# Elementwise work of a fused attention kernel, moved from VectorE to ScalarE and GpSimd

## The reference

```
x1 = x  + a_alpha * attention(ada(x))                        # 16 heads of 16
x2 = x1 + f_alpha * (silu(h @ gate) * (h @ hidden) @ out + out_b)   # h = ada(x1), hidden width 1024
u  = (x2 * scale * rsqrt(mean(x2^2) + eps)) @ up             # second layer
y  = int8_quant(val * gelu(gate)) @ ternary(down) + x2
```

## Time and profile before

| what | us |
|---|---|
| median of 3 runs | 1106.18 (1102.67 to 1108.35) |
| the profiled execution | 1105.27 |
| its span in the trace | 1103.5 |
| TensorE busy | 1032.5 (94%) |
| VectorE busy | 775.7 (70%) |
| ScalarE busy | 562.2 (51%) |
| GpSimd busy | 345.8 (31%) |

### The profile page before, as it was taken

The page is one execution under the profiler, slowest core; times in us unless marked ns, Lnnn a source line. Parts: engine busy times, 40 slices in busy tenths (PEclk is TensorE's granted clock), DMA queues, the critical chain, the costliest instruction groups (busy, mean ns, idle before and its releaser), DMA issues.

```text
span 1103.5 us, 19199 instructions
## 1 busy us (share of the span) xinstructions
PE 1032.5 (94%) x6775; PEld 719.0 (65%) x6775; DVE 775.7 (70%) x1557; ACT 562.2 (51%) x1260; POOL 345.8 (31%) x414
## 2 busy tenths in 40 slices
PE   7788799999999999999999999979989999899997
PEld 6233357746765775677577557734868888788775
DVE  5777686687669667857875786676647787466775
ACT  5357574567566555756665575555552323132221
POOL 2410142423333332324233242201332444243331
PEclk9799999999999999999999999998999999999998
DMA  8644623154153406423440623160310111002111
GB/s 265 155 99 152 93 91 122 17 102 149 59 86 98 142 2 112 126 87 48 117 141 21 112 87 107 28 142 1 97 53 29 59 58 30 29 29 63 59 53 39
DMA packets 89375, 92.71 MB, mean 84 GB/s; under 512 B 11856, under 2 KB 86616, under 8 KB 88256
## 3 DMA queue, kind: packets, MB, share of 16 engines
q1 hardware_dynamic: 87248, 89.59, 31.1%
q10 hardware_dynamic: 2032, 1.90, 0.6%
HBM read 61.68 MB, written 29.78 MB: 83 GB/s over the span
## 4 chain that ended last, share of the span: by engine, by line
PE 77%; DVE 13%; issue 5%; DMA 2%; POOL 1%; ACT 1%; SPq 0%; POOLq 0%; DVEq 0%; ACTq 0%
PE gen L1171 30%; PE core L1171 13%; PE pvb L1286 11%; PE core L1260 9%; PE core L1274 8%; DVE negmax L932 7%; PE gen L1498 2%; PE gen L1245 1%; PE pvb L1490 1%; DVE o L956 1%; PE pvb L1294 1%; DMA parts_d<-qk 1%; DMA shift_d<-shift 1%; PE gen L1324 1%; PE core L1264 1%
## 5 line engine op out<-in xcount | busy, mean ns | idle before, releaser
L932 DVE TENSOR_REDUCE negmax<-core 128x1 f32<-128x512 f32 x512 | 338.1, 686 | 166.4 <-PE core L1260 165.2
L715 ACT ACTIVATE p<-core 128x512 f32<-128x512 f32 x512 | 278.4, 597 | 142.8 <-PE core L1274 140.1
L1171 PE MATMUL gen<-hs,wgh 128*128 128x256 f32 x1536 | 220.8, 295 | 9.5 <-DVE a L989 9.5
L1260 PE MATMUL core<-kst,qst 96*128 96x512 bf16 x512 | 193.9, 395 | 33.2 <-DVE negmax L932 27.7
L1171 PEld LDWEIGHTS gen<-hs,wgh 128*128 128x128 f32 x1536 | 196.5, 190 | 28.1 <-DVE a L989 14.7
L1171 PE MATMUL core<-wup,hp 128*128 128x512 f32 x768 | 191.8, 399 | 0.9 <-POOL hp L655 0.9
L606 POOL TENSOR_TENSOR a<-a 128x256 fp32r<-128x256 f32 x128 | 94.6, 739 | 291.5 <-ACT a L733 289.0
L1171 PEld LDWEIGHTS core<-wup,hp 128*128 128x128 f32 x768 | 141.2, 190 | 29.4 <-issue 0.9
L1274 PE MATMUL core<-qst,kst 99*128 99x512 bf16 x512 | 157.1, 387 | 1.0 <-DMA qst<-shift_d 1.0
L1260 PEld LDWEIGHTS core<-kst,qst 96*128 96x128 bf16 x512 | 46.0, 97 | 149.7 <-DVE negmax L932 76.7
L1286 PE MATMUL pvb<-p,vst 128*32 128x512 f32 x1024 | 123.8, 601 | 0.0
(11 more groups left out here) (159 smaller groups left out, 1199.1 us busy)
## 6 DMA issues: line engine op xcount, KB each, us to landing
parts_d<-qk SPq DMA_DIRECT2D x30, 384.0 KB, 2.7
v_d<-v SPq DMA_DIRECT2D x8, 1024.0 KB, 3.9
vst<-v_d SPq DMA_DIRECT2D x16, 512.0 KB, 5.4
qst<-parts_d SPq DMA_DIRECT2D x96, 64.0 KB, 2.3
qst<-parts_d SPq DMA_DIRECT2D x48, 128.0 KB, 4.6
kst<-parts_d SPq DMA_DIRECT2D x48, 128.0 KB, 7.8
kst<-parts_d SPq DMA_DIRECT2D x91, 64.0 KB, 2.3
xr<-in_x_dram SPq DMA_DIRECT2D x8, 512.0 KB, 4.0
```

Source lines behind the costliest of these rows:

```text
L715: act.activation(p32[:, ring(b, m), k * S:(k + 1) * S], stb[k], ACT.Exp, scale=SCALE).then_inc(s["exp_"], 1)
L932: dve.tensor_reduce(negmax[:, n // TT, n % TT:n % TT + 1], smb[n % 2], AX_X, ALU.max, negate=True).then_inc(s["smax"], 1)
L1171: last = pe.matmul(out_, l, r, start=start and i == 0, stop=stop and i == len(passes) - 1, **kw)
L1260: pe.matmul(smb[n % 2], qst[0:KROWS, h, q * P:(q + 1) * P], kst[0:KROWS, h, :], start=True, stop=True).then_inc(s["smax_mm"], 1)
```

## The change

Five pieces are moved, and the waits with them.

1. `affine` of layer one runs on ScalarE (Identity with a scale and a bias per partition) for all batches but the first, at the same step 4, ahead of `h_hi` in ScalarE's code and behind the step's exponentials.
2. The addition of `first_residual` runs on GpSimd, one instruction for each half at steps 5 and 6. VectorE keeps the multiplication. VectorE's `qk_rest` waits for `x1_`, since it writes the buffers that GpSimd reads.
3. At step 31 ScalarE copies the feed-forward's second half from PSUM to `h32[:, 1]` (`y_out`); this raises `yt`.
4. GpSimd then multiplies it by f_alpha in place (raises `ym`, waits for it) and does the addition that it did before.
5. SyncE's wait ahead of the load of `al` is for `x2_` in place of `yt`; `turn_o` of the last batch also waits for `yt`.

```diff
@@ SyncE
-                    need_sp("yt", 2, last, 0)
+                    need_sp("x2_", 2, last, 0)
@@ GpSimd
+            def first_residual(b, c):
+                if c == 0:
+                    need(pool, "xr_load", 16, b, 16)
+                    need(pool, "x2_st", 16, b, 0)
+                need(pool, "xt_", 2, b, c + 1)
+                pool.tensor_tensor(x1[:, 2 * c:2 * c + 2, :], xt[c].rearrange("p (t d) -> p t d", t=2), xr[:, 2 * c:2 * c + 2, :], ALU.add).then_inc(s["x1_"], 1)
...
                 need(pool, "yt", 2, b, c + 1)
+                if c == 1:
+                    y = h32[:, 1, :].rearrange("p (t d) -> p t d", t=2)
+                    pool.tensor_tensor(y, y, al[:, D:2 * D].unsqueeze(1).broadcast_to([P, 2, D]), ALU.mult).then_inc(s["ym"], 1)
+                    need(pool, "ym", 1, b, 1)
...
+                    for c in range(2):
+                        for b in at(z, T_OP[c] + 1):
+                            first_residual(b, c)
@@ ScalarE
+            def affine(b):
+                need(act, "cur_set", 1, b, 1)
+                need(act, "x2_", 2, b - 3, 2)
+                for k in range(KD):
+                    need(act, "xt1", KD, b, k + 1)
+                    act.activation(h32[:, k, :], gen[XT_BANK[k]][:, :], ACT.Identity, bias=cur[:, 0, KD + k:KD + k + 1],
+                                   scale=cur[:, 0, k:k + 1]).then_inc(s["h32_1"], 1)
+            def y_out(b):
+                need(act, "y_mm", NCH, b, NCH)
+                need(act, "h32_2", KD, b, KD)
+                act.copy(h32[:, 1, :], gen[Y_BANK][:, :]).then_inc(s["yt"], 1)
...
+                    for b in at(z, T_DOWN[2 * KF - 1] + 1):
+                        y_out(b)
+                    for b in at(z, T_H1):
+                        if b > 0:
+                            affine(b)
@@ VectorE
             def qk_rest(b, j):
                 need(dve, "qk_h", 2 * KD, b, j + 1)
+                if j < 2:
+                    need(dve, "x1_", 2, b - 2, j + 1)
...
                 scaled("xt_", xt[c], gen[two_banks(b, OP_BANK)[c]], 0)
-                need(dve, "xt_", 2, b, c + 1)
-                dve.tensor_tensor(x1[:, 2 * c:2 * c + 2, :], tiles(xt[c]), xr[:, 2 * c:2 * c + 2, :], ALU.add).then_inc(s["x1_"], 1)
...
-                    for b in at(z, T_DOWN[2 * KF - 1] + 1):
-                        second_scaling(b, 1)
...
                     for b in at(z, T_H1):
-                        need(dve, "cur_set", 1, b, 1)
-                        need(dve, "x2_", 2, b - 3, 2)
-                        affine(b, 1, 0, 1, 0)
+                        if b == 0:
+                            need(dve, "cur_set", 1, b, 1)
+                            affine(b, 1, 0, 1, 0)
@@ TensorE, turn_o
+                if b == B - 1:
+                    need(pe, "yt", 2, b, 0)
```

More of the change, by code:

```diff
@@ L241, in build @@
         st_mm exp_ pv_mm o_raw o_tr o_rec o_norm
-        o_t oh ol oproj xt_ x1_ x1b sq2 ms2 rs2 xn2 xt2 h32_2 hh2 hl2
+        o_t oh ol oproj xt_ x1_ x1b ym sq2 ms2 rs2 xn2 xt2 h32_2 hh2 hl2
         gh_mm tanh_ u_ a_ ah a_lo y_mm yt x2_ x2_st
@@ L973, in first_residual @@
                     need(dve, "al_load", 16, b, 16)
-                    need(dve, "xr_load", 16, b, 16)
-                    need(dve, "x2_st", 16, b, 0)
                     need(dve, "qk_l", 2 * KD, b + 1, 2 * KD)
```

## The result

The changed kernel takes 1112.36 us in the median of 20 runs (1107.67 to 1123.52), the kernel before 1107.66 (1101.72 to 1113.05 in 19 of 20, and one of 1715.66): a ratio of 1.0051, with a 95% interval of [1.0033, 1.0069]. The measured time lies in the predicted range (1099 to 1116); the predicted 1108.2 was 4 us too low. Of these 4 us, 2.4 are the base: the prediction counts from the profiled execution's 1105.27, and the median of the kernel before is 1107.66 here. The profiled execution took 1109.41 us, 4.1 above that of before.

A forecast was written before the change was run, and what follows sets the result against it. TensorE, busy 94.97 of a 98.5 us period, was taken as the bound, with VectorE the bound around the period's start. -3.5 + 3.1 - 0.2 + 2.75 + 0.8 = +2.95 us on 1105.27 gave 1108.2 us, range 1099 to 1116.

The forecast's parts named there:

- Part 1, the gain: Scaling at step 31: VectorE's slot at the period's start comes back, 0.58 us in periods 2 to 7, -3.5 us.
- Part 1, the reload: Step 5: x2 is stored later, so TensorE waits for the shift rows' reload; 5 x 0.5 + 0.6 = +3.1 us.
- a wait in all of these periods: Sign of being wrong: TensorE's wait for the shift rows' reload appears in all periods, not in period 6 and one or two others.
- the DMAs up to 1.15 later: SyncE's queue behind x2: DMAs up to 1.15 us later, TensorE 0.58 earlier; a stall of 0 or 1.62 by period.
- the slower rival: Reload of the shift rows takes over at step 5: five periods lose 1.7 us each, 8.5 + 0.6, 1114 us; chance 0.19.
- Part 2: Scaling at step 4: the affine pair fits ScalarE's idle 1.22 us before the exponential; -0.2 us, bounds -1.4 and +0.3.
- the rival of 18 us: Table loads around each affine on ScalarE: 2 x 1.28 x 7 = 18 us, 1126 us; chance 0.03.
- Part 3: Additions of steps 5 and 6 on GpSimd: squares start 0.62 us later; +2.75 us, bounds -0.6 and +0.62 a period.
- Both delays overlap: +0.3 to +0.4: VectorE's wait for the root and a late score product overlap in periods 1 to 6: 6 x 0.35 = 2.1 us.
- Part 4: Start of the second layer: the last period's addition on GpSimd ends later, past a slack of 0.34; +0.8 us, once.
- The third rival: GpSimd's two new instructions meet VectorE's shift-row casts at step 2: 1.2 us in six periods, 7 us, 1115 us; chance 0.04.
- The first rival: VectorE's relief comes back wherever it is in the chain of waits, new chains hidden: 9.3 us, 1096 us; chance 0.16.

The follow-up runs named there:

- e4: The changed kernel with SyncE's V load issued behind the store and reload of the shift rows; 4.5 to 5.4 us faster than the change at equal clock.
- e1: The kernel before with only the affine of step 4 moved to ScalarE, except batch 0; +0.2 +-0.7 us at equal clock.
- e2: The kernel before with only the additions of steps 5 and 6 moved to GpSimd; +4.2 +-0.8 us at equal clock.
- f_after: The whole change, unaltered, timed again in another series; the change's two equal-clock figures against the kernel before are +4.8 and +5.7 us.
- e3: The kernel before with only pieces 3 to 5, the feed-forward's last scaling on ScalarE and GpSimd; +2.1 us at equal clock.
- f9: The change with both additions and batch 6's last scaling back on VectorE, and the V load behind the shift rows; ratio 0.9937 to the kernel before.
- e7: The kernel before with only SyncE's V load moved behind the shift rows; -1.5 +-0.7 us at equal clock.
- e8: The change with V load behind the shift rows, step 6's addition and batch 6's last scaling on VectorE; the last edit won 1.0 +-1.0 us at equal clock.

## Why the prediction held, and where it was too low

**Part 1, the gain.** Right: 0.6 us in each of six periods (a stand of 0.66 for 1.25).

**Part 1, the reload.** The sum of the named waits came out, +3.07 net for +3.1, and that the reload is the place, e4 proves. But the prediction named a wait in all of these periods as a sign that it is wrong, and all six wait, by 0.15 to 1.49. The 0.5 a period was a choice between 0 and 1.6, and that the mean of periods 2 to 6 is 0.51 is luck: I had periods like 5 with 1.72 us of room and no wait, periods like 6 with 1.62 of waiting, and they waited 0.49 and 0.36. The step that failed is "the DMAs up to 1.15 later". Against the turn of `o` the forecast makes that at most 1.73, and the reload came 2.36 later in period 5 and 0.59 in period 6. The V load between x2's store and the shift rows was mentioned as traffic ahead, where it was what stretched the one and could be moved; the remedy was not in my text. The term also left out what follows such a wait, 0.17 a period. With it the reload costs 4.1 us, where I had 3.1 and the slower rival, by the same mechanism, 9.1.

**Part 2.** Right: e1 gives +0.2 +-0.7. The pair takes 1.45 us, not 1.1 to 1.2, and still fits. In period 0 the wait of the earlier trace rows has become one for the exponential, as forecast. No table load came with it: the two on ScalarE are those of before, at the squares and the gelu.

```profile
L713 ACT ACT_TABLE_LOAD x1 | 1.3, 1283 | 2.8 <-issue 2.8
L899 ACT ACT_TABLE_LOAD x1 | 1.3, 1283 | 2.0 <-PE core L1201 2.0
```

So the trace agrees with the rule of the Trainium skill (ScalarE: Activation LUTs, Table sets: the hidden batching unit) that identity is in every set, and the rival of 18 us is out.

**Part 3.** Mechanism right, size too low; the term that was mis-sized is "Both delays overlap: +0.3 to +0.4". Squares came 0.62 later by my sum and 0.58 later at `norm_t` in the trace (14.94 to 15.52); I took half of that to overlap with the exponentials, and 0.15 does. The term is 0.43 a period in e2, and at equal clock the piece costs 4.2 +-0.8 where I had 2.75; six periods of 0.43 are 2.6 of that. `norm_t` waits 0.38 for `xn`, where I named 0.5 or more as a sign. The delay of 0.58 nearly reached the upper bound of 0.62, since every link behind the squares was a wait of its own already.

The Trainium skill (GPSIMD Engine Reference, Elementwise — side-by-side cycle accounting) has GpSimd's additions at about twice VectorE's time. Here it is 1.26 to 0.69, a factor of 1.8, so the direction agrees.

**Part 4.** +1.1 for +0.8. The multiplication and addition take 1.26 and 1.40: the second meets VectorE's work there. The first tile's rows, GpSimd and TensorE:

```profile
824.00 1.40 POOL L607 TENSOR_TENSOR x<-h,x 128x512 f32<-128x512 f32 x1
...
827.14 1.17 PE L1201 MATMUL core<-wup,hp 128*128 128x512 f32 x4 [1.76 <-POOL hp L670]
```

**The sum** by measured terms: -3.6 + 3.1 + 1.0 (0.17 in six) + 2.6 (0.43 in six) + 1.1 = +4.2, period 7's share of piece 2 not counted, against the +4.8 to +5.7 measured and the +2.95 forecast. What it lacks can lie in period 7. The forecast's terms there were -0.58 + 0.6 + 0.65, +0.7 us; the period takes 97.11 us in the change and 96.32 in f_after, at the same mean clock of 0.96 as the 94.88 before, so +2.2 and +1.4. Which of the pieces does that stays open, for in e1 to e3 its clock was another. The third rival stayed out: GpSimd's instructions at 626.12 to 628.7 end before VectorE's casts at step 2, by 0.2 us and not by 1. The first rival, relief wherever VectorE is in the chain, did not come true: VectorE's relief on the additions is worth nothing, since TensorE did not wait for it.

## What to carry to other kernels

Before work leaves a busy engine, ask of each piece alone whether anything waits for it, and what the next reader of its result waits for: one piece (step 31) was worth moving once the reload no longer paid for it (f9 lies 3 us below e7 at equal clock, and e3 2 us above the kernel before), one (the affine) made no difference, and one (the additions) lengthened a chain in which every link already waited. When a producer gets slower, read the issuing queue behind it and move what isn't urgent out of the way; exchanging two lines on SyncE gave back all that this change had lost. Give the kernel before the same exchange, or the gain of the one is taken for that of the other. And compare times of a per cent or less at equal mean clock too, or else an unlucky series refutes a right theory; what the clock itself owes to the kernel stays outside that comparison.

## What the runs showed of the hardware

- TensorE's granted clock, averaged over an execution, lay between 0.972 and 0.986 in 33 runs of the kernel before in one series, and that goes with most of the scatter of 3 us: 0.87 us of span per 0.001.
- In single stretches it fell to the lower level where TensorE had stood more than elsewhere: before the first turn of `o`, in period 7, behind the waits near 940 us, but not in each execution. Period 7 took 95.40 us in e8 and 92.78 in f9; TensorE stood still for about 9 us in both, and its mean clock there was 0.95 and 0.98.
- ScalarE's Identity with a scale and a bias per partition, 128x512 from PSUM, takes 0.79 us, and two of them in a row 1.45; its plain copy 0.59.
- A small cast of 16x128 on VectorE took 0.21 us, and 1.16 beside GpSimd's `qk_parts`; in the kernel before it was 0.82. GpSimd's `h_lo` went from 1.45 to 1.28 us an instruction in the mean when VectorE's addition beside it was gone.
- From the issue of the shift rows' store to that of their reload it took 4.8 to 5.7 us in periods 2 to 6 of the change, with a V load of 512 KB issued ahead, and 3.6 to 4.1 in e4 without. In the kernel before it was 3.7 to 5.4, and 2.2 to 3.2 in e7.
